# A memset between the dispatch scatters of a mixer and mixture-of-experts kernel

## The reference

```python
x = _layernorm(x + _L0_attn_ref(x, ...))      # input projection, 4-tap convolution, long convolution, gate, output projection
# _L0_ffn_ref:
gate_logits = jnp.einsum('bsd,ed->bse', x, gate_w) + gate_b + expert_bias
top_idx = jnp.argmax(gate_logits, axis=-1)
for e in range(NUM_EXPERTS):
    mask = (top_idx == e)[..., None].astype(x.dtype)
    h = jax.nn.relu(jnp.einsum('bsd,df->bsf', x, w1[e]) + b1[e])
    y = jnp.einsum('bsf,fd->bsd', h, w2[e]) + b2[e]
    out = out + mask * y
x = _layernorm(x + out)
```

## Time and profile before

| what | value |
|---|---|
| median of 3 runs | 289.91 us (286.74 to 290.55) |
| profiled execution, its own time | 286.29 us |
| its span, first to last instruction | 284.6 us |
| busy: TensorE, ScalarE, VectorE, GpSimd | 246.3, 189.9, 174.1, 127.1 us |
| dispatch scatters, L554 | 32, 959 ns each |
| scatters to out, L588 | 39, 989 ns each |

### The profile page before, as it was taken

How to read it: one execution, slowest core, us unless ns; L and a number is a source line. 1 busy time by engine, 2 the same in 40 slices (tenths; PEclk the granted TensorE clock), 3 DMA queues, 4 the chain that set the end, 5 groups by cost and what they waited for, 6 DMA issues and landing times.

```text
span 284.6 us, 8826 instructions
## 1 busy us (share of the span) xinstructions
PE 246.3 (87%) x2757; PEld 220.5 (77%) x2758; DVE 174.1 (61%) x555; ACT 189.9 (67%) x526; POOL 127.1 (45%) x152
## 2 busy tenths in 40 slices
PE   4799999999979899999798797473989999999960
PEld 1588888888867688888698696363989899999950
DVE  2789993999364455556246448630686567666652
ACT  3979999926998688887455152403766767777730
POOL 6000000400049799996244746474025455455445
PEclk9999999999999999999999959955899999999996
DMA  6729877400299999995843201713656666777400
GB/s 217 217 88 368 323 273 284 163 0 0 74 323 317 307 295 322 318 316 153 322 148 87 82 29 58 223 50 87 187 159 175 192 201 170 225 201 201 130 31 5
DMA packets 54267, 52.06 MB, mean 183 GB/s; under 512 B 4415, under 2 KB 42817, under 8 KB 54114
## 3 DMA queue, kind: packets, MB, share of 16 engines
q1 hardware_dynamic: 51506, 46.65, 54.0%
q0 software_dynamic: 2304, 4.34, 4.3%
q10 hardware_dynamic: 432, 0.79, 0.8%
HBM read 38.14 MB, written 14.07 MB: 183 GB/s over the span
## 4 chain that ended last, share of the span: by engine, by line
PE 53%; ACT 17%; DVE 16%; issue 8%; another core or an unknown queue 2%; POOL 2%; DMA 1%; DVEq 0%; ACTq 0%; SPq 0%; POOLq 0%
PE banks L1449 11%; PE banks L1439 11%; PE banks L1332 7%; PE banks L1397 6%; ACT BR L645 4%; PE banks L1342 4%; PE banks L1346 4%; PE banks L1395 3%; ACT Z L624 2%; PE banks L1319 2%; ACT RE L635 2%; PE banks L1380 2%; ACT CR L608 2%; DVE CR L961 2%
## 5 line engine op out<-in xcount | busy, mean ns | idle before, releaser
L1261 PE MATMUL banks<-Wx,XT 128*128 128x256 f32 x256 | 62.2, 388 | 1.4 <-DVE Wx L845 1.4
L507 POOL TENSOR_TENSOR Wx<-BR,RE 128x384 f32 (+1 forms) x32 | 47.7, 1520 | 28.7 <-PE banks L1261 26.1
L588 POOL DMA_INDIRECT out<-X x39 | 38.6, 989 | 48.6 <-issue 26.7
L782 ACT ACTIVATE Z<-banks,BR 128x128 f32<-128x128 f32 x156 | 44.8, 373 | 22.5 <-PE banks L1439 13.1
L1261 PEld LDWEIGHTS banks<-Wx,XT 128*128 128x128 f32 x256 | 49.6, 194 | 10.1 <-DVE Wx L845 3.0
L1439 PE MATMUL banks<-Z 128*128 128x128 f32 x312 | 44.6, 289 | 6.0 <-ACT Z L771 4.4
L1439 PEld LDWEIGHTS banks<-Z 128*128 128x128 f32 x312 | 40.5, 203 | 7.8 <-ACT Z L771 4.8
L1449 PE MATMUL banks<-BR,Z 128*128 x312 | 42.4, 280 | 2.4 <-DVE X L1190 2.4
L554 POOL DMA_INDIRECT dispatched_rows<-TR,CR x32 | 30.7, 959 | 26.9 <-DVE CR L1115 18.2
L1449 PEld LDWEIGHTS banks<-BR,Z 128*128 128x128 f32 x312 | 38.8, 196 | 2.9 <-issue 2.9
L1190 DVE TENSOR_TENSOR X<-banks,X 128x128 f32<-128x128 f32 x39 | 11.3, 290 | 24.9 <-PE banks L1449 20.9
(11 more groups left out here) (215 smaller groups left out, 460.9 us busy)
## 6 DMA issues: line engine op xcount, KB each, us to landing
TR<-kernel_rows SPq DMA_DIRECT2D x32, 512.0 KB, 6.2
Z<-w SPq DMA_DIRECT2D x39, 256.0 KB
dispatched_rows<-TR SPq DMA_DIRECT2D x3, 2310.0 KB, 8.6
X<-dispatched_rows SPq DMA_DIRECT2D x39, 66.0 KB
XT<-hidden_t SPq DMA_DIRECT2D x10, 256.0 KB, 3.8
RE<-decay_and_turns SPq DMA_DIRECT2D x2, 1024.0 KB, 7.2
BR<-w SPq DMA_DIRECT2D x1, 2048.0 KB, 8.1
dispatched_rows<-TR SPq DMA_DIRECT2D x1, 1848.0 KB, 7.1
```

Of the source, the lines that this page charges most:

```text
L507: nc.gpsimd.tensor_tensor(BC[:, k, 0:LAGS, :].rearrange("p m (s r n) -> p (m s) r n", s=STRIPS, r=2), Btab[:, :, :, :, :, one].rearrange(" ...
L588: pool.indirect_dma_start(out_rows, bass.IndirectOffsetOnAxis(XS[:, n % ROWS_RING, TOKEN_COL:TOKEN_COL + 1].bitcast(U32), 0), F[:, slot, : ...
L782: last = nc.scalar.activation(HT[:, j, c * P:c * P + P], bank[UP_BANKS[j]][:, c * P:c * P + P], ACT.Relu, bias=B1[:, bass.ds(experts[j] * ...
L1261: last = mm(bank[X_BANKS[k]][:, j * CHAN:(j + 1) * CHAN], XT[:, slot, at:at + CHUNK], Wx[:, tap, :], start=(tap == 0), stop=(tap == TAPS - 1))
```

## The change

Ahead of each of the 32 dispatch scatters GpSimd zeroes 512 columns of `pause`, a scratch region that nothing reads, and waits until this has ended before it issues the scatter. The memset comes behind the quad's wait for its places, so that a quad has four memsets, the first one ahead of its first scatter. Nothing else changes.

```diff
+        pause = RW[:, 2560:3072]
...
+        s_pause = sem("pause_over")
...
                     for k in range(4):
+                        nc.gpsimd.memset(pause, 0.0).then_inc(s_pause, 1)
+                        pool.wait_ge(s_pause, n * 4 + k + 1)
                         pool.indirect_dma_start(slots_dram, bass.IndirectOffsetOnAxis(pos[:, batch, k:k + 1], 0),
                                                 X1[:, batch, k, :], None).then_inc(s_sc[batch], 16)
```

## The result

The changed kernel takes 278.81 us (median of 4 runs, 276.9 to 283.28), beside 288.87 us (286.74 to 290.55) for the kernel before in the same session: the ratio is 0.973 with an interval of 0.966 to 0.980. By either reading the change gains 8 to 10 us. The forecast was 297.1 us with a range from 288 to 304 us, so the prediction was wrong in sign and its range doesn't hold the time. The profiled execution of the changed kernel is its slowest one, 283.28 us with a span of 281.6 us; the spans of the other three are 275.1 to 278.9 us, so the trace shows less of the gain than the times do.

A forecast was written before the change was run, and what follows sets the result against it. GpSimd's 32 dispatch scatters were taken to gate the first blocks and block 12. A period of 2.30 us makes block 12's rows 7.2 us late: 289.9 + 7.2 = 297.1 us, range 288 to 304 us.

The forecast's parts named there:

- The period: Time from one GpSimd dispatch scatter's start to the next: 2.30 us with memset and wait, 1.04 us more than before.
- The two rows on which the choice rested: Two GpSimd scatter starts after a wait, 0.77 and 0.86 us on, taken as showing the full start-up.
- When GpSimd is through: End of GpSimd's dispatch: scatter number 32 starts at 217.75 us instead of 194.69 us, 23 us later.
- The first blocks: TensorE's first `down` starts at 201.9 us instead of 198.75 us, 3.15 us later, because scatter 20 comes late.
- The held signals: TensorE's signals or matmuls possibly held up by dense scatters; 4.25 us at the first block, counted as gone.
- Block 12: Deciding wait: block 12's rows arrive at 224.1 us, against TensorE's transpose at 216.86 us now, 7.2 us later.
- 6.33 us: From the last dispatch scatter's start to block 12's rows: first scatter to `out`, its landing and SyncE's load.
- The break-even of 2.07 us: Scatter period under which the change wins, as block 12's rows are then there at 216.86 us as now.
- signals set free, start-up hidden: Faster rival: start-up overlaps the memset, period 1.79 us, `down` 6.6 us earlier, 283.3 us; chance 0.12.
- the only unexplained wait: ScalarE's 5.86 us wait, put down to remote, for first-block matmuls whose rows had ended; spoke for the faster rival.
- The fall of the clock behind a wait of TensorE: Slower rival: after TensorE's 4.1 us wait at block 12's transpose the clock halves, costing 3.4 us, 300.5 us; chance 0.20.
- The rule on PE and ACT: Skill sentence that PE and ACT never wait on anyone; by it wider spacing wins nothing and the faster rival has no chance.

The follow-up runs named there:

- e2: Changed kernel with the memset cut from 512 to 8 columns, wait kept; ratio 1.000 to the kernel before of its session.
- e8: Changed kernel plus a memset and wait ahead of each of the first 8 scatters to `out`; ratio 1.042 to the kernel before (268.3 us).
- e18: Changed kernel plus memset and wait ahead of each of the first 8 scatters to `out`, where the kernel before takes 286.1 us; ratio 0.993.
- e9: Kernel before, unchanged, run again for its trace in a session where it takes 267.7 us; ratio 0.997.
- e4: Changed kernel with the memset lengthened from 512 to 1024 columns; ratio 1.023 to the kernel before (286.3 us).
- e10: Changed kernel, no further edit, in a session where the kernel before takes 267.7 us; ratio 1.020.
- e1: Changed kernel run again, no further edit; 281.52 us beside 286.27 us for the kernel before, ratio 0.976.
- e15: Kernel before with the last 12 dispatch scatters replaced by memsets of 1024 columns, three quads' rows left out; ratio 0.974 (before 286.2 us).
- e3: Changed kernel whose scatter no longer waits for its memset, the memset waiting for the previous memset; 275.16 us, ratio 0.964 to the kernel before.

## Why the prediction was wrong

**The period: the step that failed.** It took 0.77 us for a scatter's start after a wait, none of it hidden, and 1.04 us for the whole addition. Measured are 0.28 us and 0.52 us (and 0.01 us, not 0.04 us, from a scatter to its memset); the period is 1.79 us and not 2.30 us. That is the lower bound which the same part gave (start-up hidden, 1.79 us) and then set aside. Of the 18.3 us between 297.1 and 278.8 us this step accounts for 13.8 us: with 1.79 us the prediction's own working gives 283.3 us. The two rows on which the choice rested both stand behind an idle GpSimd: L578 is the first indirect DMA at all, and L554 at 145.86 us follows 7.78 us of waiting. Neither is a scatter behind a memset in a running row. e2 shows both cases side by side, 0.70 us from the memset's start for the first scatter, 0.28 us from its end for the rest. What decides between the two figures stays open. Being idle isn't all of it: in e8 and e18 the scatters to `out`, in a running row, start 0.79 us behind their memset, which is nearly what the prediction took.

**When GpSimd is through.** The counting was right and inherited the period: with 1.79 us it gives 201.9 us for the last dispatch, measured 201.68 us.

**The first blocks.** The prediction gave `down` at 192.2 us for a period of 1.79 us; measured is 190.30 us. The held signals were seen in the earlier trace rows, but counted at one place, with 4.25 us. This is the second term that was too small: they were also in the quads (places of the last quad 9.6 us later than in the changed kernel) and in the later blocks, and the same kernel in a session without them is 17.2 us shorter (e9).

**Block 12.** The path was right: where the dispatch ends late, block 12's rows come last (e4, e10). In the changed kernel they cost TensorE only 0.35 us of waiting. The last dispatch plus 6.33 us gives 220.3 us in e4 (220.36), 208.0 us in the changed kernel (208.47), 207.5 us in e10 (208.92). So the sum is 0.1 to 1.5 us short, and it has luck in it: of its 6.33 us, 0.77 us are the start-up of the first scatter to `out`, which measured 0.30 us, so that landing and load took 0.5 to 1.9 us more than the 4.6 us counted. In e1, whose TensorE stood still beside the scatters to `out`, the transpose is later (212.07 us) than the sum says (208.3). The break-even of 2.07 us for the period is not contradicted: 1.79 us is faster, 2.21 us is slower where signals are held. Where they aren't, TensorE is there at 203.93 us instead of 216.86 us, and the same arithmetic makes 1.79 us a loss, which e10 shows.

**The rivals and chances.** What came true is the rival "signals set free, start-up hidden", with 283.3 us and 0.12; it was 4.5 us too high. It had the only unexplained wait of the trace for it, against two rows that were both read behind an idle GpSimd. The range ended at 288 us and left this case out. The fall of the clock behind a wait of TensorE was seen, but at the scatters to `out`, not at block 12's rows.

**The rule on PE and ACT.** The Trainium skill, SBUF — State Buffer, "Who interferes with whom", says "PE and ACT never wait on anyone", and the prediction let this rule out any gain. That section is about the engines' ports to SBUF, and no run here shows such a port at work. What was late is something else: ScalarE was released 4.25 us behind the end of its matmul, and not where memsets stood in for the scatters (e15). So the sentence speaks neither for nor against the gain, and the prediction read too much into it.

**What stays open.** What sets the level of a session; it isn't the chip's number. What inside the chip delays the signals and spreads out TensorE's own work, and whether the issue or the transfers of the scatters do it. Why the changed kernel's runs spread over 6 us (276.9 to 283.28) while its profiled executions were the slowest ones both times; their stall beside the scatters to `out` may be missing in the shorter ones, but no trace of one exists. And the version without the wait (e3) wasn't run on the lower level; worked out from e9 and the 6.33 us it would have block 12's rows at 204.2 us, 0.3 us behind TensorE (and up to 1.5 us later still, as in e10), and its first blocks a little late, so an estimate is no gain and a loss of 0 to 2 us.

## What to carry to other kernels

If an engine waits for TensorE although TensorE's rows have ended, look at what GpSimd issues at that time: in sessions in which signals were held, a gap of 0.7 us between indirect scatters set them free here, 0.4 us did nothing, and it can be had without a wait. Put gaps first where nothing waits for the scatters: the last 12 paused gave 1.6% on one level and cost nothing on the other, while pauses among those on which the first blocks wait cost 2.5% wherever the signals weren't held. And price a start-up from a row in which the engine was as busy as it will be and issued the same DMA; where no such row exists, as here, keep both bounds open. Last, a gain measured in one session can be a loss in another: 0.973 and 1.020 are the same two kernels.

## What the hardware did that I hadn't expected

The release of engines that wait for TensorE comes up to 6 us late while GpSimd issues indirect scatters 0.30 or 0.40 us apart (worked out from the rows: 4.25, 6.0 and 4.9 us in the kernel before, the last for the count that L1108 takes at 165.36 us; 5.2 and 4.3 us beside the scatters to `out` of the changed kernel). At 0.54 us the waits are shorter, at 0.70 us and more none was seen. TensorE's own matmuls are spread out at the same time (3.72 against 1.12 us for eight transposes). This is so in sessions in which the kernel before takes 286 to 289 us, and it isn't in those with 268 us, with identical code and a trace that shows the same 0.96 us scatters. And a wait for a memset ahead of a dispatch scatter costs 0.11 us in a running row (0.28 against 0.17 us behind the memset's end), while the scatter starts 0.60 us behind an 8-column memset when GpSimd had been idle (e2; behind the first 512-column one, also after an idle GpSimd, it is 0.28 us), and a scatter to `out` 0.79 us behind its memset even in a running row (e8, e18).
